# Message stage of a graph network layer: pair products from bf16 one-hots and edge weights in three bf16 pieces

## What is computed

```python
Hb = jnp.einsum('ni,bio->bno', h, V)                 # V: 4 basis matrices
coef = w_comp[etype]                                 # edge -> 4 coefficients
m = sum(coef[:, b][:, None] * Hb[b][src] for b in range(4))
m = m * norm[:, None]                                # norm: the edge weight
agg = jax.ops.segment_sum(m, dst, num_segments=n_nodes)
hn = relu(agg + h @ loop_w + bias)
y = hn @ ffn_w.T + ffn_b + h                         # then a layer norm
```

## Time and profile before

| | |
|---|---|
| median of 3 runs | 2160.6 us (2160.43 to 2161.55) |
| the profiled execution: its own time | 2160.85 us |
| the profiled execution: first to last instruction | 2158.8 us |
| PE busy | 2068.8 us (96%) |
| DVE busy | 1516.5 us (70%) |
| ACT busy | 1271.0 us (59%) |
| POOL busy | 671.9 us (31%) |
| granted TensorE clock, mean | 0.992 of full |
| line 804 (sums), 2500 matmul records | 580.7 us |
| line 792 (pair products), 6300 matmul records | 403.7 us |

### The profile page before, as it was taken

The page is one execution under the profiler, slowest core; times in us unless marked ns, Lnnn a source line. Parts: engine busy times, 40 slices in busy tenths (PEclk is TensorE's granted clock), DMA queues, the critical chain, the costliest instruction groups (busy, mean ns, idle before and its releaser), DMA issues. The chain is left out here.

```text
span 2158.8 us, 53995 instructions
## 1 busy us (share of the span) xinstructions
PE 2068.8 (96%) x19640; PEld 1667.4 (77%) x19640; DVE 1516.5 (70%) x4205; ACT 1271.0 (59%) x2225; POOL 671.9 (31%) x814
## 2 busy tenths in 40 slices
PE   1799999999999999999989999999998999999998
PEld 1688888888888888888865777777775677777776
DVE  2777788788778878878736666666664667667665
ACT  0466666666666666666644555655563565555664
POOL 3656466556646655664300000000000000000000
PEclk9899999999999999999999999999999999999999
DMA  3011111111111111111113212222111222222220
GB/s 74 11 45 52 50 37 56 52 39 47 52 49 37 59 49 39 47 52 47 42 57 117 90 64 86 89 89 87 64 57 61 95 97 96 96 75 86 95 96 8
DMA packets 43154, 137.13 MB, mean 64 GB/s; under 512 B 9196, under 2 KB 24490, under 8 KB 36615
## 3 DMA queue, kind: packets, MB, share of 16 engines
q1 hardware_dynamic: 38614, 128.31, 16.5%
q0 software_dynamic: 4400, 6.80, 1.3%
HBM read 91.89 MB, written 43.20 MB: 63 GB/s over the span
## 5 line engine op out<-in xcount | busy, mean ns | idle before, releaser
L804 PE MATMUL ps<-matrixT,x_rows 125*128 125x256 f32 (+1 forms) x2500 | 580.7, 383 | 1.7 <-ACT aggT L893 1.7
L874 ACT COPY matrixT<-ps 125x500 f32<-125x500 f32 (+2 forms) x800 | 395.7, 583 | 244.3 <-PE ps L792 241.2
L804 PEld LDWEIGHTS ps<-matrixT,x_rows 125*128 125x128 f32 x2500 | 459.2, 190 | 69.3 <-issue 2.2
L1499 ACT COPY weightsT_l<-ps 125x500 f32<-125x500 f32 (+1 forms) x450 | 234.0, 543 | 368.9 <-PE ps L1420 368.9
L1577 DVE CUSTOM_DVE_ANT_0 scores_l<-ps,bias_rows_l 125x500 f32<-125x500 f32 (+1 forms) x700 | 396.8, 619 | 41.2 <-issue 40.0
L792 PE MATMUL ps<-high_weights,low_onehot 64*125 64x125 f32 x6300 | 403.7, 278 | 12.2 <-ACT matrixT L874 6.6
L792 PEld LDWEIGHTS ps<-high_weights,low_onehot 64*125 64x125 f32 x6300 | 365.9, 188 | 46.4 <-issue 29.1
L1420 PEld LDWEIGHTS ps<-eye,scores_l 125*125 125x125 f32 x2500 | 301.0, 189 | 115.6 <-issue 97.3
L1420 PE MATMUL ps<-eye,scores_l 125*125 125x125 f32 x2500 | 364.1, 286 | 4.6 <-ACT scores_l L1481 3.4
L1585 DVE COPY weightsT_l<-ps 125x500 f32<-125x500 f32 (+1 forms) x250 | 150.1, 600 | 269.7 <-PE ps L1420 267.3
L1481 ACT ACTIVATE scores_l<-scores_l,neg_max_l 125x1500 f32<-125x1500 f32 x200 | 320.9, 1605 | 20.2 <-DVE neg_max_l L1614 20.2
(11 more groups left out here) (148 smaller groups left out, 1614.6 us busy)
## 6 DMA issues: line engine op xcount, KB each, us to landing
bias_rows_l<-bias SPq DMA_DIRECT2D x50, 1562.5 KB, 6.6
bias<-bias SPq DMA_DIRECT2D x75, 500.0 KB, 2.6
x_rows<-in_x SPq DMA_DIRECT2D x1, 1562.5 KB
bias<-bias SPq DMA_DIRECT2D x25, 62.5 KB, 1.6
x<-x_rows SPq DMA_DIRECT2D x25, 62.5 KB
x_rows_l<-x SPq DMA_DIRECT2D x25, 62.5 KB
out<-rows_l SPq DMA_DIRECT2D x25, 62.5 KB
dst_int<-in_dst SPq DMA_DIRECT2D x1, 402.8 KB
```

What stands on the lines that cost most here:

```text
L804: last = nc.tensor.matmul(psG[:, BASES * SPLIT * side:BASES * (SPLIT * side + SIDE[side])], x[:, h, :], MT[side][:, 0:SIDE[side], BASES * ...
L874: last = nc.scalar.copy(MT[side][:, at:at + 2 * c - 1:2, 0:COLS], psP[bank][0:R, :].rearrange("p (i c) -> p i c", c=128)[:, 0:c, 0:COLS])
L1499: nc.scalar.copy(PT[i % 8][:, 0:cw[c]], psT[i % 2][0:R, 0:cw[c]]).then_inc(z["pa_ok"], 1)
```

## The change

`own` (the flag that a slot belongs to the node) is coded as 128 rather than 512, so that every digit is an integer below 256 and exact in bf16. Both one-hots and the digits become bf16. Each coefficient w is cut into three bf16 pieces: HI = bf16(w), MID = bf16(w - HI), LO = bf16(w - HI - MID). `high_weights` then holds 13 columns for each high digit (LO, MID, HI of four coefficients, and the count). The product of a slot pair becomes three bf16 products for each of its two nodes that add up in the same PSUM bank: HI with the count (125 columns), MID (100) and LO (100). In PSUM and in `matrixT` the five values of a high digit now stand together (`WIDE` = 5) rather than 100 weights and then 25 counts.

To let four slots stand side by side (`QUAD` = 4), both tiles are laid out with the slot innermost: neighbouring columns of a matmul operand are four bf16 elements, 8 bytes, apart.

DVE's build has four operations instead of three: high one-hot (200 elements), low one-hot (1000), and two products of 1200 elements, in place of 200, 1000 and 800; the seventh slot buffer is no longer cut off in the last period. New are `rest_of_weights` and `low_weights` on DVE (256 elements each, once a tile) and one copy on ACT (256 elements). New waits: ACT's MID copy for `rest_ok` (DVE), DVE's `low_weights` for `mid_ok` (ACT), the first build of a tile for `lo_ok`, PE's `turn_codes` for the last tile's `rest_ok`.

```diff
-OWN = 512.0
+OWN = 128.0
+PIECE = 3
...
-        digitsT = [sb(f"digitsT{i}", [128, 2, PAIRS], F32) for i in range(2)]
-        weightsT = [sb(f"edge_weightsT{i}", [128, PAIRS, BASES], F32) for i in range(2)]
-        L = sb("low_onehot", [128, BUFS, GROUP, R], F32)
-        Hw = sb("high_weights", [128, BUFS, GROUP, 128], F32)
+        digitsT = [sb(f"digitsT{i}", [128, 2, SLOTS], BF16) for i in range(2)]
+        weightsT = [sb(f"edge_weightsT{i}", [128, PIECE * BASES, SLOTS], BF16) for i in range(2)]
+        rest = sb("weights_rest", [128, BASES, SLOTS], F32)
+        L = sb("low_onehot", [128, BUFS, GROUP // QUAD, R, QUAD], BF16)
+        Hw = sb("high_weights", [128, BUFS, GROUP // QUAD, T, PIECE * BASES + 1, QUAD], BF16)
...
+            def rest_of_weights(s, par):
+                v.wait_ge(codesT_ok, s + 1)
+                if not is_int(s) or s >= 1:
+                    v.wait_ge(mid_ok, s)
+                turned = psK[:, 0:PLANES * SLOTS].rearrange("p (c n) -> p c n", n=SLOTS)
+                V.tensor_tensor(rest[:, :, :], turned[:, 2:PLANES, :], weightsT[par][:, HI, :], ALU.subtract).then_inc(rest_ok, 1)
+            def low_weights(s, par):
+                v.wait_ge(mid_ok, s + 1)
+                V.tensor_tensor(weightsT[par][:, LO, :], rest[:, :, :], weightsT[par][:, MID, :], ALU.subtract).then_inc(lo_ok, 1)
...
-                    v.wait_ge(codesT_ok, s + 1)
+                    v.wait_ge(lo_ok, s + 1)
...
-                V.tensor_tensor(Hw[:, at, 0:p, 0:BASES * T].rearrange("p n (h b) -> p n h b", b=BASES),
-                                hots.unsqueeze(3).to_broadcast([128, p, T, BASES]),
-                                weightsT[par][:, to, :].unsqueeze(2).to_broadcast([128, p, T, BASES]),
-                                ALU.mult).then_inc(built, 1)
+                for g in range(quads):
+                    pairs = slice(GROUP * k + QUAD * g, GROUP * k + QUAD * (g + 1))
+                    last = V.tensor_tensor(Hw[:, at, g, :, 0:COUNT, :],
+                                           Hw[:, at, g, :, COUNT, :].unsqueeze(2).to_broadcast([128, T, COUNT, QUAD]),
+                                           weightsT[par][:, :, pairs].unsqueeze(1).to_broadcast([128, T, COUNT, QUAD]), ALU.mult)
+                last.then_inc(built, 1)
...
                 for k in range(PERIODS):
+                    if k == PERIODS - AHEAD and inside(w + 1):
+                        rest_of_weights(w + 1, par)
...
+                    if k == PERIODS - AHEAD and inside(w + 1):
+                        low_weights(w + 1, par)
...
                 for i in range(size(k)):
-                    for q in range(2):
-                        own = slice(SLOTS * q, SLOTS * (q + 1))
-                        last = nc.tensor.matmul(psP[2 * (i // 4) + q][0:R, 128 * (i % 4):128 * (i % 4) + COLS], L[own, at, i, :],
-                                                Hw[own, at, i, 0:COLS], start=True, stop=True)
+                    g, j = i // QUAD, i % QUAD
+                    for piece in (HI_COUNT, MID, LO):
+                        for q in range(2):
+                            own = slice(SLOTS * q, SLOTS * (q + 1))
+                            to = psP[2 * g + q][0:R, 128 * j:128 * j + COLS].rearrange("p (h c) -> p h c", c=WIDE)
+                            last = nc.tensor.matmul(to if piece == HI_COUNT else to[:, :, 0:BASES], L[own, at, g, :, j],
+                                                    Hw[own, at, g, :, piece, j], start=(piece == HI_COUNT), stop=(piece == LO))
...
-                        nc.scalar.copy(weightsT[par][:, :, :],
-                                       turned[:, 2:PLANES, 0:PAIRS].rearrange("p c n -> p n c")).then_inc(codesT_ok, 1)
+                        nc.scalar.copy(weightsT[par][:, HI, :], turned[:, 2:PLANES, :]).then_inc(codesT_ok, 1)
...
+                    if k == 5 and inside(w + 1):
+                        act.wait_ge(rest_ok, w + 2)
+                        nc.scalar.copy(weightsT[par][:, MID, :], rest[:, :, :]).then_inc(mid_ok, 1)
```

More of the change, by code:

```diff
@@ L35 @@
 PLANES = 2 + BASES
-COLS = (BASES + 1) * T
+WIDE = BASES + 1
+COLS = WIDE * T
+QUAD = 4
 GROUP, PERIODS, BUFS, AHEAD = 8, 8, 4, 2
@@ L457, in message @@
         codes = [sb(f"codes{i}", [128, PLANES, SLOTS], F32) for i in range(2)]
-        digitsT = [sb(f"digitsT{i}", [128, 2, PAIRS], F32) for i in range(2)]
-        weightsT = [sb(f"edge_weightsT{i}", [128, PAIRS, BASES], F32) for i in range(2)]
-        L = sb("low_onehot", [128, BUFS, GROUP, R], F32)
-        Hw = sb("high_weights", [128, BUFS, GROUP, 128], F32)
+        digitsT = [sb(f"digitsT{i}", [128, 2, SLOTS], BF16) for i in range(2)]
[3 more added lines that the diff above has]
+        Hw = sb("high_weights", [128, BUFS, GROUP // QUAD, T, PIECE * BASES + 1, QUAD], BF16)
+        own_lows = sb("own_lows", [128, R, QUAD], BF16)
+        highs = sb("highs", [128, T, QUAD], BF16)
+        LO, MID, HI = (slice(BASES * i, BASES * (i + 1)) for i in range(PIECE))
+        HI_COUNT, COUNT = slice(BASES * 2, BASES * PIECE + 1), BASES * PIECE
         MT = [sb(f"matrixT{i}", [R, SPLIT, 128], F32) for i in range(2)]
@@ L675, in build_hot @@
[L675 to L678, removed]
[L679 to L683 removed]
+                quads = GROUP // QUAD
@@ new lines, in build_hot @@
+                own = digitsT[par][:, 0, to].rearrange("p (g i) -> p g i", i=QUAD).unsqueeze(2).to_broadcast([128, quads, R, QUAD])
+                high = digitsT[par][:, 1, to].rearrange("p (g i) -> p g i", i=QUAD).unsqueeze(2).to_broadcast([128, quads, T, QUAD])
+                V.tensor_tensor(Hw[:, at, :, :, COUNT, :], highs[:, :, :].unsqueeze(1).to_broadcast([128, quads, T, QUAD]),
+                                high, ALU.is_equal).then_inc(hot, 1)
+                V.tensor_tensor(L[:, at, :, :, :], own_lows[:, :, :].unsqueeze(1).to_broadcast([128, quads, R, QUAD]),
+                                own, ALU.is_equal)
@@ L776, in turn_codes @@
                     pe.wait_ge(codesT_ok, s)
+                    pe.wait_ge(rest_ok, s)
                 for c in range(PLANES):
                     for q in range(2):
-                        last = nc.tensor.matmul(psK[SLOTS * q:SLOTS * (q + 1), SLOTS * c:SLOTS * c + PAIRS], codes[par][:, c, :],
-                                                eye[:, q:2 * PAIRS:2], start=True, stop=True)
+                        last = nc.tensor.matmul(psK[SLOTS * q:SLOTS * (q + 1), SLOTS * c:SLOTS * (c + 1)], codes[par][:, c, :],
+                                                eye[:, q:128:2], start=True, stop=True)
                 last.then_inc(codes_ps, 1)
@@ L804, in sums @@
                     last = nc.tensor.matmul(psG[:, BASES * SPLIT * side:BASES * (SPLIT * side + SIDE[side])], x[:, h, :],
-                                            MT[side][:, 0:SIDE[side], BASES * h:BASES * (h + 1)], start=(h == 0), stop=(h == T - 1))
+                                            MT[side][:, 0:SIDE[side], WIDE * h:WIDE * h + BASES], start=(h == 0), stop=(h == T - 1))
                 if hi == T:
@@ L884, in counts_out @@
                 nc.scalar.copy(CT[:, lo:hi, SPLIT * side:SPLIT * side + SIDE[side]],
-                               MT[side][:, 0:SIDE[side], BASES * T + lo:BASES * T + hi].rearrange("p n h -> p h n")).then_inc(
+                               MT[side][:, 0:SIDE[side], WIDE * lo + BASES:WIDE * hi:WIDE].rearrange("p n h -> p h n")).then_inc(
                                    (ctA_ok, ctB_ok)[side], 1)
```

15 lines of the change are left out of this document (7 added, 8 removed).

## The result

The changed kernel takes **2433.7 us** (median of 4 runs, 2432.3 to 2434.6), the kernel before 2160.5 us in the same comparison: a ratio of 1.126, interval 1.124 to 1.128. The forecast was 2078 us with a range up to 2240. It was wrong, in sign too.

What follows compares the result with a forecast made beforehand. PE's stream was taken to bound the message stage. Pair products 2.8 plus switches 0.75, less 0.1 each for ACT and DVE, gave 3.35 us a tile, 84 over 25 tiles, 1 back: 83 us, so 2078 us, range 2052 to 2240.

Steps and rivals of the forecast that it cites:

- The step of three bf16 products: PE's pair products: three steps at the transposes' 0.057 us make a slot pair 0.171 us against 0.215, gaining 2.8 us a tile.
- The argument against spaced operands: PE's line 779: moving `eye`, already spaced by 8 bytes, takes 0.065 us for 63 float32 columns, near 0.054.
- The rival of the spaced operands: PE's pair products: 8-byte spacing holds all three steps at 0.108, 0.324 us a slot pair, 2313 us; chance 0.08.
- Its sign in the profile: PE's records in the changed kernel: if the spaced operands are slow, HI's records are as long as MID's.
- The scattered output: PE's MID and LO writing four of five PSUM columns: steps at 0.108, 0.273 us a slot pair, 2234 us; chance 0.08.
- The switches: Uncovered weight loads at both ends of PE's bursts: some 0.05 us less at each end, 0.75 us a tile gained.
- ACT's give-back: PE at period 0 waits for ACT's evacuation, which had 0.37 us of slack: some 0.1 us a tile lost.
- DVE at two elements a cycle: DVE's build with bf16 operands: 2.2 us after the change, against 2.30 before; 4.0 at one element a cycle.
- the 0.1 us a tile set down for DVE: PE's wait for DVE's builds: 0.2 us in tiles with least slack, on average 0.1 us a tile lost.
- Its working: DVE's lag by period 4: PE forward 2.5 us, start 1.0 late, five faster builds; put at 1.5 against 1.29 slack.

Runs made afterwards that it cites:

- both_flat: Changed kernel with both operands of the pair products read contiguously, the moving one from a tile filled with 1.0: 2137.4 us.
- packed_one_product: Three bf16 pieces as in the changed kernel, but contiguous operands pair by pair, PSUM order of before, one 2400-element DVE product a period: 2110.8 us, ratio 0.9769.
- before_wide: Float32 kernel before, with columns of high_weights, PSUM banks and matrixT ordered as in the changed kernel: 2207.6 us, ratio 1.0217.
- weights_flat: Changed kernel with only the stationary operand of the pair products read as one contiguous run: 2419.5 us.
- moving_flat: Changed kernel with only the moving operand of the pair products read as one contiguous run, from a tile filled with 1.0: 2402.1 us.
- after_full_rows: Changed kernel with each pair product reading all 128 partitions in place of 64: 2947.3 us.
- spacing_4_bytes: Changed kernel with QUAD = 2 in place of 4, so elements of both operands lie 4 bytes apart in place of 8: 2261.6 us.

## Why the prediction was wrong, point by point

- **The step of three bf16 products (0.171 us a slot pair): this failed.** It was 0.367. The 0.057 us came from transposes whose operands are contiguous, and I carried it over to operands 8 bytes apart. `both_flat` and `packed_one_product` show the 0.057 to be right for contiguous operands (0.175 a slot pair) and the spacing to be the whole difference.
- **The argument against spaced operands.** I held line 779 against them: its `eye` is spaced by 8 bytes and 63 columns take 0.065 us, "near" the 0.054 of float32. That is 1.03 ns a column, or 0.96 by the starts of its records, 60 ns apart; the changed kernel's columns cost 1.0. The row had nearly the whole price of a column in it. I read it as a ratio to float32 (1.2), when a cost of fetching stays in nanoseconds while the product under it gets twice as fast. This reading fits both rows, and bursts at half the clock bear it out (last section); no run here takes the spacing away from a float32 product.
- **The rival of the spaced operands (2313 us, chance 0.08)** was the right mechanism. Its slot pair of 0.324 was 0.043 too small (68 us), and the sums were missing (47 us): 2428, against 2434 measured. With a known row at about 1 ns a column it deserved the largest chance, and the range ended 73 us below it. Its sign in the profile was put wrongly too: HI's records were to be as long as MID's, but the cost goes by columns, 324 against 290 ns.
- **The sums: a term that was not there.** The change to `WIDE * h` moves no work, so I priced it at nothing without looking at where the runs start. `before_wide` shows 47 us for it.
- **The scattered output (2234 us): wrong.** The steps of `both_flat`, with scattered output, and of `packed_one_product`, without, are the same within 1 ns. Both go at the pace of the weight load, 58 ns, so a few ns a step for the output could hide under it. The Trainium skill, "PSUM — Partial Sum Buffer", section "Specifications (TRN2)", has any non-contiguous pattern slow matmuls significantly; for writes of four float32 columns in five at 58 ns a step these runs disagree.
- **The switches (0.09 us a burst with its loads) were right:** burst and switch together became 0.42 us shorter in `packed_one_product`, 0.44 was forecast. In the changed kernel they are lost in the longer burst.
- **ACT's give-back (0.1 us a tile) was right in size:** 9.0 less 6.6 us in 25 tiles. The wait of the sums for `aggT`, 6 us more in the fast kernels, was not foreseen.
- **DVE at two elements a cycle was right.** A build of the changed kernel lasts from 611.32 to 613.55, 2.2 us as forecast:

```profile
611.32 0.26 DVE L700 TENSOR_TENSOR high_weights<-highs,digitsT 128x200 bf16<-128x200 bf16 x1
611.49 0.67 DVE L702 TENSOR_TENSOR low_onehot<-own_lows,digitsT 128x1000 bf16<-128x1000 bf16 x1
612.08 1.47 DVE L707 TENSOR_TENSOR high_weights<-high_weights,edge_weightsT 128x1200 bf16<-128x1200 bf16 x2
```

  The 1000 elements took 1.19 us in float32. The Trainium skill, "VectorE: DVE Perf Modes", section "The perf-mode tier table", has this, and the trace agrees. In `both_flat`, which has the changed kernel's DVE work and PE near the forecast pace, PE waits only 4.3 us for `high_weights`, against 5.6 before: the 0.1 us a tile set down for DVE did not come. Its working did not add up either, since its terms (2.5 + 1.0 - 0.5) make 3.0 us and not 1.5.
- **The sum without the two misses:** `both_flat` less the 47 us of the sums is 2090, against 2078. The rest of the working held to 12 us, of which 6 are `aggT`.

## What to carry to other kernels

A faster type shortens a product only as far as its operands arrive: before pricing it, write down the byte distance of neighbouring elements in the moving and in the stationary operand, and take the pace from a row with that distance, in nanoseconds an element and not as a ratio. When two transfers overlap, taking away either cost alone shows next to nothing, so test both together before both are acquitted. And a layout chosen for one engine (runs of four for DVE) has to be priced at each of the others that read it; here DVE's speed could be had with contiguous operands, and the same idea was then 2.3% faster and not 12.6% slower.

## What the runs showed of the hardware

- **Spacing of TensorE's bf16 operands.** Neighbours 2, 4 and 8 bytes apart in both operands: 175, 255 and 367 ns for three steps of 125, 100 and 100 columns. At 8 bytes the columns alone cost about 1.0 ns each plus 14 (`weights_flat`), the load of 125 columns of weights alone 117 ns (`moving_flat`), and a step takes the longer of the two, within 3 ns (MID and LO take 114 in the changed kernel). The Trainium skill, "SBUF — State Buffer", section "Specifications (TRN2)", asks for two hits in each 16-byte line for full bandwidth, and adds that each crossing to a new line pays a penalty. By the first half elements 8 bytes apart, two to a line, would come at full pace; these runs show less than half of it.
- **The pace of spaced operands does not follow TensorE's clock.** A burst of `after_full_rows` takes 6.12 us at a granted clock of 0.50 (1.2 GHz), and 6.10 at 1.00 (2.4 GHz, shown above). A burst of `packed_one_product`, with contiguous operands, takes 2.80 us at 0.50 and 1.60 at 1.00. The rows at 0.50, first `after_full_rows`, then `packed_one_product`:

```profile
66.78 6.12 PE L827 MATMUL ps<-high_weights,low_onehot 128*125 128x125 bf16 x48 [2.20 <-ACT matrixT L909]
```
```profile
64.72 2.80 PE L827 MATMUL ps<-high_weights,low_onehot 64*125 64x125 bf16 x48 [2.21 <-ACT matrixT L910]
```

  That fits a pace set by fetching the operands, and not one set by the array.
- **Runs of four float32 in the moving operand** cost 38 ns more a record (255 in place of 216, 256 columns) when they start 4 or 12 bytes past a multiple of 16, and 4 ns when 8 past it.
- **Products on the two halves of the rows run side by side** in float32 and bf16: the same 32 records take 2.01 us on both halves and 3.75 on one.
- **An instruction of DVE with four free dimensions** (pairs, pieces, digits, bases) on its bf16 operands kept two elements a cycle (about 0.6 ns each): 2400 in 1.40 us. Runs of two in the products of `spacing_4_bytes` did not, though its compares with runs of two did (1000 in 0.67 us): the same 2400 in four instructions take 2.44 us, 1.0 ns each. What in their layout costs this was not tried.
- **DVE beside POOL.** The same operations of `packed_one_product` while POOL does little (at 616 to 619 us: one operation of 125 x 1 until 617.28) and while it works on `coef_parts` and `codes` almost without a break (at 624 to 632 us):

```profile
616.16 0.68 DVE L700 TENSOR_TENSOR high_weights<-highs,digitsT 128x1008 bf16<-128x1008 bf16 x1
617.35 1.40 DVE L707 TENSOR_TENSOR high_weights<-high_weights,edge_weightsT 128x2400 bf16<-128x2400 bf16 x1
...
626.05 1.93 DVE L707 TENSOR_TENSOR high_weights<-high_weights,edge_weightsT 128x2400 bf16<-128x2400 bf16 x1
628.86 1.51 DVE L700 TENSOR_TENSOR high_weights<-highs,digitsT 128x1008 bf16<-128x1008 bf16 x1
```
```profile
625.66 1.05 POOL L550 TENSOR_TENSOR coef_parts<-coef_parts 128x256 f32<-128x256 f32 x1
628.77 1.06 POOL L549 TENSOR_TENSOR coef_parts<-kinds,comp 128x512 f32<-128x512 f32 x1
```

  The compare of 1008 elements takes 1.51 us there in place of 0.68, though not each time: over the run its median is 0.93 us where POOL is busy for over 90% of it, and 0.68 where POOL is idle. It is in such stretches that PE waits (0.84 us at 633.14). That POOL is the cause was read from this coincidence and not tried.
